# One PSUM bank per head's scores, and first scores issued ahead of second ones, in the first attention

## The reference

```
qkv  = x @ qkv_w + qkv_b                  # 16 heads of 8 channels
attn = softmax(q @ k.T * 8 ** -0.5)       # per group and head: 512 x 512
out  = (attn @ v) @ proj_w + proj_b
```

## Time and profile before

| | us |
|---|---|
| median of 3 runs | 3276.28 |
| lowest and highest run | 3265.56, 3277.72 |
| profiled execution, its span | 3286.4 |
| attention's first scores begin | 434 |
| attention's end | about 1300 |

### The profile page before, as it was taken

The page is one execution under the profiler, slowest core; times in us unless marked ns, Lnnn a source line. Parts: engine busy times, 40 slices in busy tenths (PEclk is TensorE's granted clock), DMA queues, the critical chain, the costliest instruction groups (busy, mean ns, idle before and its releaser), DMA issues. The chain is left out here.

```text
span 3286.4 us, 46340 instructions
## 1 busy us (share of the span) xinstructions
PE 2885.2 (88%) x15778; PEld 1733.9 (53%) x15778; DVE 2521.8 (77%) x6150; ACT 1771.8 (54%) x2711; POOL 920.1 (28%) x885
## 2 busy tenths in 40 slices
PE   6999869999999997999976698899899999989853
PEld 4666523444444433666654465566566656656432
DVE  6998778888888861899967898776466687797765
ACT  3545317777777774455445456464344555655444
POOL 2212122111111101122101455565223323434233
PEclk9999959999999995999985789899899999999875
DMA  4434332212212201343420000000000000000000
GB/s 130 101 83 104 81 106 86 98 54 95 87 66 95 86 22 43 88 105 88 95 53 1 1 14 20 13 26 20 33 7 14 14 14 7 14 7 26 7 7 26
DMA packets 71604, 167.20 MB, mean 51 GB/s; under 512 B 8793, under 2 KB 9417, under 8 KB 67145
## 3 DMA queue, kind: packets, MB, share of 16 engines
q1 hardware_dynamic: 69192, 160.04, 16.9%
q10 hardware_dynamic: 2176, 4.19, 0.3%
HBM read 120.68 MB, written 43.52 MB: 50 GB/s over the span
## 5 line engine op out<-in xcount | busy, mean ns | idle before, releaser
L710 DVE TENSOR_REDUCE att_mx<-att_pair 128x2 f32<-128x1024 f32 x512 | 617.2, 1220 | 122.7 <-PE att_pair L960 122.6
L886 ACT ACTIVATE att_pt<-att_pair 128x1024 f32<-128x1024 f32 x512 | 522.7, 1025 | 226.1 <-PE att_pair L970 223.8
L982 PE MATMUL att_o<-att_pt,att_vx 128*32 128x256 f32 x4096 | 329.1, 406 | 10.1 <-ACT att_oT L892 5.1
L960 PE MATMUL att_pair<-att_k,att_q 32*128 32x512 f32 x1024 | 266.6, 524 | 50.5 <-DMA att_k<-att_spread_k 14.9
L970 PE MATMUL att_pair<-att_q,att_k 32*128 32x512 f32 x1024 | 261.7, 512 | 0.0
L970 PEld LDWEIGHTS att_pair<-att_q,att_k 32*128 32x128 f32 x1024 | 97.2, 188 | 190.7 <-issue 165.2
L960 PEld LDWEIGHTS att_pair<-att_k,att_q 32*128 32x128 f32 x1024 | 98.4, 191 | 140.3 <-ACT att_pt L886 92.5
L460 ACT ACTIVATE ffnA_h<-ffnA_up,b 128x512 f32<-128x512 f32 x144 | 98.9, 688 | 131.2 <-PE ffnA_up L105 130.7
L460 ACT ACTIVATE ffnB_h<-ffnB_up,b 128x512 f32<-128x512 f32 x144 | 98.7, 686 | 130.4 <-PE ffnB_up L105 129.9
L982 PEld LDWEIGHTS att_o<-att_pt,att_vx 128*32 128x32 f32 x4096 | 90.8, 110 | 140.1 <-issue 120.2
L1908 ACT ACTIVATE att1k_sq<-att1k_k 128x512 f32<-128x512 f32 x128 | 76.2, 595 | 163.0 <-PE att1k_k L105 162.8
(11 more groups left out here) (535 smaller groups left out, 7691.5 us busy)
## 6 DMA issues: line engine op xcount, KB each, us to landing
ffnA_weights<-ffnA_weights SPq DMA_DIRECT2D x128, 256.0 KB, 5.1
att_q<-att_spread_q SPq DMA_DIRECT2D x16, 1024.0 KB, 4.9
att_k<-att_spread_k SPq DMA_DIRECT2D x16, 1024.0 KB, 4.8
att_spread_q<-att_qhi SPq DMA_DIRECT2D x32, 256.0 KB, 2.5
att_spread_k<-att_khi SPq DMA_DIRECT2D x32, 256.0 KB, 3.3
twk_hi<-ffnB_weights SPq DMA_DIRECT2D x32, 256.0 KB, 3.8
twk_lo<-ffnB_weights SPq DMA_DIRECT2D x32, 256.0 KB, 5.1
tgk_hi<-ffnB_weights SPq DMA_DIRECT2D x32, 256.0 KB, 6.1
```

The source lines that it names most:

```text
L710: v.tensor_reduce(top[b % 2][:, t, h:h + 2], pair("s", k)[:, :].rearrange("p (h n) -> p h n", h=2), AX, ALU.max, negate=True).then_inc(mx, 1)
L886: a.activation(pt[k % 8][:, :, :].rearrange("p h n -> p (h n)"), pair("t", k)[:, :], ACT.Exp, scale=scale).then_inc(p_, 1)
L960: last = pe.matmul(pair("s", k)[:, (j - j0) * 512:(j - j0 + 1) * 512], qb[b % 3][r, u, t * P:(t + 1) * P], kb[b % 3][r, u, :], start=True, ...
L982: last = pe.matmul(obank[j * BLOCK:(j + 1) * BLOCK, cols], vxb[b % 3][:, t, 4 * u + j, :], pt[(2 * g + j // 2) % 8][:, j % 2, cols], start ...
```

## The change

The six banks are no longer three pairs for both kinds. First scores get three single banks `s0` to `s2`, second scores three single banks `t0` to `t2`, each bank holding one head's 512 columns. Every matmul of scores waits for its own bank and raises the counter itself; VectorE and ScalarE take one head's 512 columns at a time, two instructions where there was one. Counters that counted pairs now count heads, so the waits on them are doubled. In TensorE's order the next loop's first scores now stand ahead of the second scores.

```diff
-    banks = [mem.ps(f"pair{i}", 1024) for i in range(3)]
+    sbanks, tbanks = [mem.ps(f"s{i}") for i in range(3)], [mem.ps(f"t{i}") for i in range(3)]
...
-            v.wait_ge(s_, k + 1)
-            v.tensor_reduce(top[b % 2][:, t, h:h + 2], pair("s", k)[:, :].rearrange("p (h n) -> p h n", h=2), AX, ALU.max, negate=True).then_inc(mx, 1)
+            for n in (2 * k, 2 * k + 1):
+                v.wait_ge(s_, n + 1)
+                v.tensor_reduce(top[b % 2][:, t, h + n % 2:h + n % 2 + 1], sbanks[n % 3][:, :], AX, ALU.max, negate=True).then_inc(mx, 1)
...
-            v.wait_ge(mx, STEPS * (b + 1))
+            v.wait_ge(mx, 2 * STEPS * (b + 1))
...
-                sp.wait_ge(t_, STEPS * (b - 2))
+                sp.wait_ge(t_, 2 * STEPS * (b - 2))
...
-            a.wait_ge(t_, k + 1)
...
-            a.activation(pt[k % 8][:, :, :].rearrange("p h n -> p (h n)"), pair("t", k)[:, :], ACT.Exp, scale=scale).then_inc(p_, 1)
+            for n in (2 * k, 2 * k + 1):
+                a.wait_ge(t_, n + 1)
+                a.activation(pt[k % 8][:, n % 2, :], tbanks[n % 3][:, :], ACT.Exp, scale=scale).then_inc(p_, 1)
...
-            pair_free(pe, "s", k)
             for j in (j0, j0 + 1):
...
+                n, r = 2 * k + j - j0, slice(BLOCK * j, BLOCK * (j + 1))
+                if n >= 3:
+                    pe.wait_ge(mx, n - 2)
+                pe.matmul(sbanks[n % 3][:, :], qb[b % 3][r, u, t * P:(t + 1) * P], kb[b % 3][r, u, :], start=True, stop=True).then_inc(s_, 1)
...
-            pair_free(pe, "t", k)
             for j in (j0, j0 + 1):
...
+                n, r = 2 * k + j - j0, slice(BLOCK * j, BLOCK * (j + 1))
+                if n >= 3:
+                    pe.wait_ge(p_, n - 2)
+                pe.matmul(tbanks[n % 3][:, :], kb[b % 3][r, u, t * P:(t + 1) * P], qb[b % 3][r, u, :], start=True, stop=True).then_inc(t_, 1)
...
-            pe.wait_ge(p_, 2 * g + 2)
+            pe.wait_ge(p_, 4 * g + 4)
...
+                if STEPS * m + n + 1 < total:
+                    scores(STEPS * m + n + 1)
                 if 0 <= k < total:
                     again(k)
-                if STEPS * m + n + 1 < total:
-                    scores(STEPS * m + n + 1)
```

More of the change, by code:

```diff
@@ L625, in attn0 @@
     xg = lambda b: X[:, b, :, :]
[L626 to L629, removed]
     def place(k):
@@ L634, in place @@
         return b, n // 8, n % 8 // 2, n % 2 * 2
[L636 to L643, removed]
     def uses_of_misc():
@@ L956, in scores @@
                 pe.wait_ge(dk[b % 3], 16 * (b // 3 + 1))
-            pair_free(pe, "s", k)
             for j in (j0, j0 + 1):
-                r = slice(BLOCK * j, BLOCK * (j + 1))
-                last = pe.matmul(pair("s", k)[:, (j - j0) * 512:(j - j0 + 1) * 512], qb[b % 3][r, u, t * P:(t + 1) * P], kb[b % 3][r, u, :], start=True, stop=True)
-            last.then_inc(s_, 1)
+                n, r = 2 * k + j - j0, slice(BLOCK * j, BLOCK * (j + 1))
+                if n >= 3:
+                    pe.wait_ge(mx, n - 2)
+                pe.matmul(sbanks[n % 3][:, :], qb[b % 3][r, u, t * P:(t + 1) * P], kb[b % 3][r, u, :], start=True, stop=True).then_inc(s_, 1)
         def again(k):
@@ L966, in again @@
                 pe.wait_ge(dm[b % 3], 64 * (b // 3 + 1))
-            pair_free(pe, "t", k)
             for j in (j0, j0 + 1):
-                r = slice(BLOCK * j, BLOCK * (j + 1))
-                last = pe.matmul(pair("t", k)[:, (j - j0) * 512:(j - j0 + 1) * 512], kb[b % 3][r, u, t * P:(t + 1) * P], qb[b % 3][r, u, :], start=True, stop=True)
-            last.then_inc(t_, 1)
+                n, r = 2 * k + j - j0, slice(BLOCK * j, BLOCK * (j + 1))
+                if n >= 3:
+                    pe.wait_ge(p_, n - 2)
+                pe.matmul(tbanks[n % 3][:, :], kb[b % 3][r, u, t * P:(t + 1) * P], qb[b % 3][r, u, :], start=True, stop=True).then_inc(t_, 1)
         def weigh(w, t, h):
```

## The result

| | before | changed |
|---|---|---|
| median, us | 3270.92 (4 runs, 3265.38 to 3277.72) | 3299.86 (4 runs, 3291.87 to 3307.64) |
| ratio, 95% interval | | 1.009 (1.0062 to 1.0117) |
| profiled execution, span | 3286.4 | 3305.0 |

The change makes the kernel 0.9% slower. 0.5% faster had been forecast, 3260 us, with a range of 3249 to 3268 and a wider one up to 3290.

What follows compares the result with a forecast made beforehand. First scores waiting for exps in one ring of three pairs were taken as the bound. Steady part -32.6, start +12.9 and end +3 gave -16.7 us: 3260 us, forecast range 3249 to 3268, 8 in 10 range 3236 to 3290.

Steps and rivals of the forecast that it cites:

- The bound of before: Steady attention groups: first scores wait for exps in a ring of three pairs; ten of 49.83 us are TensorE waits.
- pieces 0.60 apart: VectorE's 512-column reductions last 0.68 us but start 0.60 apart, so 1.20 us a loop for 1.13.
- VectorE as the new bound: Steady group: VectorE's floor is 42.7 us, with only 0.12 us of slack in a loop.
- the four stalls at loops 9 to 17: VectorE stalls: q's projection 0.94 us, double weighing 0.31, k's projection 0.37, v's projection 0.97.
- The walk: Steady group worked through its 32 loops: stalls sum to 4.75 us, giving 47.5 us for 49.83.
- The start: First scores alone, before second scores begin: +12.9 us, from dearer reductions and from stalls at projections and transpositions.
- the halves' 2.9: First scores alone: 42 loops at 0.07 us more for two reductions in place of one, +2.9 us.
- The end: Last 42 loops of second scores and weighings: +3 us, from full-clock loops of 1.19 us and ScalarE's two pieces.
- TensorE's clock: Rival, chance 0.12: short idles in each loop lower the steady part's clock; a tenth of loops low gives 3293 us.
- the dearer halves: Rival, chance 0.10: each reduction piece costs 0.68 us, a group takes 50.4 us, total 3305 us.
- small remainders: Steady group: the last 0.23 us of the 4.75 us of VectorE stalls; `divided` lies beside each transposition of outputs.
- -32.6: Steady part, 500.9 to 1213.5 us: 2.3 us less in each of fourteen groups, a shade less for the last.

Runs made afterwards that it cites:

- the halves alone: Kernel before, pairs and order kept, with each reduction and each exp made in two pieces of 512 columns: 3295.18 us, ratio 1.0049.
- both edits: Changed kernel, first scores ahead, with the output bank's copy ahead of the exps and the moments at loop 27: 3259.87 us, ratio 0.9952.

## Why the prediction was wrong

**Right.** The bound of before and its removal; pieces 0.60 apart; VectorE as the new bound, and the four stalls at loops 9 to 17 one by one. The banks alone give 47.73 for 47.5, but that is partly luck: the walk was for first scores ahead, where a full-clock group took 48.27 with the moments moved and 47.4 only with moments and copy moved. Against the halves the prediction had set the Trainium skill, "VectorE: DVE Perf Modes", section "The DRAIN you can't avoid"; the same paragraph adds that an operation which isn't held starts earlier, and the 0.60 between starts agrees with that. The start: +10.8 for +12.9, through the named stalls (0.86 and 1.82 us), and six banks take them away, 12 us by the medians; the halves' 2.9 in it was too high, 1.8 by the run of the halves alone. The end was not right: the next stage begins 22.4 us late where the last maxima were 24.4 late, so -2 for +3.

**The step that failed** is the one that let the new group run at the full clock. "TensorE's clock" stood as a rival with 0.12, argued away with more work per microsecond. What came in its place are low stretches in all fourteen groups, 104 us of 707, behind waits of 0.57 to 1.13 us that the turned order made. Waits that VectorE's own work covers, as the one for the copy after loop 29, had been put at 0; TensorE stood idle in them all the same. The rival's own sum was good. A wholly low group of 71 us that costs 23 more is 0.33 for each low microsecond; measured are about 0.3, in single groups 0.2 to 0.4. The 104 us, less some 30 that they cost, are the work of 1.5 groups, and it had 1.45, a tenth of the loops. Its 3293 lies 7 us under the median. The 3305 of the dearer halves lies 5 above, by luck: the pieces were 0.60 apart.

**The second step** was to cost the turned order at nothing. The walk had second scores leave together with the second head's first scores, and counted their lateness only through VectorE's next stall. At loop 31 it had for `divided` at most the 0.23 us of small remainders; the group of 834.09 has some 0.5 there, and one at the low clock 1.2. In the 42.1 us that the order costs over fourteen groups, the part that is wait at the full clock is 48.27 - 47.73 = 0.54 a group, 7.6 us. Three long casts and three long additions beside GpSimd's residual bias take some 5 more. The remaining 29 or so are the 104 us at the low clock, again about 0.3 for each. This split is worked out, with the moments' move taken as worth nothing at the full clock (47.67 for 47.73 with second scores ahead); that the order causes the whole of 42.1, in the profiled executions, is shown.

**Sum.** Forecast -32.6 + 12.9 + 3 = -16.7. In the profiled executions: steady part +13.6 (of which -28.5 for the banks and +42.1 for the order), start +10.8, end -2, and -3.8 in later stages: +18.6. The medians differ by 28.9.

**Open**: what exactly makes the clock fall. Moments, copy and order each take part of the idle time away and each brings the clock nearer to 1.00, but with both edits and first scores ahead six groups still have a low stretch, with no idle time above 0.11 us on TensorE's record in the 6 us before any of them, although TensorE's busy share there (47.04 of 47.40) is higher than with second scores ahead (46.66 of 47.73), where none has. So the busy share of a group doesn't tell the two apart. Nor is the order a guarantee: with second scores ahead, six banks at the start and the moments at loop 27 two neighbouring groups had 4.8 and 2.1 us at the low clock, and four groups of the halves alone had 3.4. Open too is how much of the loss goes back to GpSimd's addition, as no run moved it alone. The Trainium skill, "TensorE: Matmul & The Clock Gate", section "A second HAM failure mode: psum-queue depth-cycling", says that short idles of TensorE between groups of matmuls, from cycling banks, can make the clock oscillate; the changed kernel agrees (0.93), the banks alone, with the same ring, do not (1.00).

## What to carry to other kernels

Where an engine works through one order, put what has a free buffer ahead of what must wait: a wait in front holds the whole chain behind it. Where the chain can be moved forward instead, as the copy here, the order costs little (3263.99 for 3263.47). When a buffer is split into smaller pieces, count how much work the ring still holds ahead; it is that which covers a projection of 1 us, not the number of banks. A plan that leaves TensorE idle at several places has to be priced at the lower clock as well. And an edit that moves one operation also moves what waits for it on other engines: look there for what it newly meets.

## What the runs showed of the hardware

- A reduction of 512 columns from PSUM lasts 0.68 us and is followed by the next 0.60 us after its start, also over 42 in a row; an instruction more costs 0.07 us.
- A cast of 64 columns on VectorE takes 0.20 to 0.38 us, but 0.96, 1.02 and 1.22 where GpSimd's 1.27 us addition on SBUF begins before it (833.75 and 834.09); an addition of 64 columns takes 0.27, but 1.26 and 1.27 there. Each ends within 0.1 us of GpSimd's end.
- Five groups in a row took 51.16 to 51.22 us with about 10.2 us each at the low clock, which fell each time some 4.3 us before the group's end. In these groups VectorE, late by the low clock, reached the maxima only as GpSimd's addition ended (cast at 986.00, addition from 985.03 to 986.31), and none of its operations there is long. Why the fall kept repeating isn't shown.
